# 8-bit weights transposed by VectorE in 32x32 squares where they are rounded, stored so, and loaded straight into one weight tile

## The chip, the cores and the metric

One core of a Trainium2 chip runs the whole program. The metric is device microseconds of that core. The engines are TensorE (PE in the rows; PEld is its weight load), VectorE (DVE), ScalarE (ACT), GpSimd (POOL) and SyncE (SP, which here only issues DMAs and waits).

## The reference

Four layers of cross attention and feed-forward (FFN) on x of 8 sequences x 100 rows x 512, everything in float32. What matters here is the third layer (L2). Its attention part is a recurrence over the context whose result is one 512-vector per sequence, and its FFN rounds weights and activations to 8-bit floats in blocks of 32 along the last axis:

```python
def _mx_dequant(t):
    blocks = t.reshape(rows, feat // 32, 32)
    scales = jnp.maximum(jnp.max(jnp.abs(blocks), axis=-1) / 448.0, 1e-30)
    q = (blocks / scales[..., None]).astype(jnp.float8_e4m3fn).astype(jnp.float32)
    return (q * scales[..., None]).reshape(rows, feat)
def _mx_linear(x2d, w):
    return _mx_dequant(x2d) @ _mx_dequant(w).T
gate, up = _mx_linear(x2d, gate_w), _mx_linear(x2d, up_w)      # gate_w, up_w: 2048 x 512
out = _mx_linear(silu(gate) * up, down_w)                      # down_w: 512 x 2048
```

A weight is rounded in blocks along the axis that the matmul sums over, and TensorE wants that axis on the partitions. So the weights are rounded with this axis along the free dimension and transposed between rounding and use.

## The kernel before

The three weights (12 MB) are cut on the host into 16 **triples** of 128 x 1536: a 128 x 512 piece of the gate, of the up and of the down weight. Class `Triples` rounds them half a triple (128 x 768) at a time, beside stages whose matmuls set the pace: nine triples beside the experts of the first layer (`stage_L0_experts`, 700 to 947 us, names beginning with `e_`), seven beside the spline FFN of the second (`stage_columns_ffn`, 1319 to 1466 us, names `f_`). For half n, DVE takes the blocks' largest values (`scales`, L2685 to L2687), POOL multiplies by the inverse (L2720), DVE takes the exponent (`power`, L2692), ACT lifts it (L2706), DVE rounds by adding and subtracting (`rounding`, L2699 and L2700), and POOL multiplies back in place (`finish`, L2713). DVE's order in the spline FFN is, in each turn of a loop over 16 pairs: two products (L2888) that PE's matmuls and ACT's silu wait for, then `power`, `scales` of the next half, `rounding`. SyncE stores each rounded triple to the DRAM tensor `rounded` (L2675), waits until it is stored, and loads the next into its place (three buffers).

`stage_L2_recurrence` (1466 to 1519 us) adds the recurrence's result to the eight sequences and normalises them. DVE does sequence i in the parts `first`, `shifted`, `second` (L3228, waits for `added`, which ACT makes at L3190 from a PE bank) and `third` (L3239, which completes the sequence and signals `res_made`); SyncE then copies the sequence's rows into the row tiles `s_rows` of the next stage (`into_tiles`, L2080). Beside it the rounded triples come back: SyncE loads a triple into one of four buffers (two named `l_early`, two `l_triple`), PE transposes it in 12 pieces (`turn`, L3308), ACT copies each bank of four into the weight tiles `s_wgu` and `s_wd` (L3200), and SyncE may load the next triple when PE has turned the one before it in the buffer. ACT's one queue holds both the 48 copies and the eight `add_shift` (L3190), in the order that the list `ADD_AT` gives. PE also makes eight `summary` matmuls (L3316) and transposes the last row tile, which DVE has rounded in the recurrence (32 rows, `s_lead`).

Each `nc.Block` ends with a barrier of all engines. The next block, `stage_ffn` (names `f_`, 1519.9 us on), begins with `gate_up(0)` on `s_lead` and the weights (L2217). SyncE meanwhile loads weights of the last layer (L3348). Everything after it depends on this stage.

Of the kernel before, what the change touches and what calls it, by code (L numbers as in the profile page):

```python
# [7 lines left out]
F32 = mybir.dt.float32  # L8
# [8 lines left out]
P = 128  # L17
# [1155 lines left out]
def stage_L0_experts(k, moe, ahead, w_gate, w_up, w_down, raw, rows8, *weights8):  # L1173
# [6 lines left out]
    with ExitStack() as ctx:  # L1180
# [12 lines left out]
        stepped = sem("dve_steps")  # L1193
        b_x, b_g, b_u, b_m, b_y = k.bank[0:2], k.bank[2:4], k.bank[4:6], k.bank[6], k.bank[7]
# [5 lines left out]
        with nc.Block() as block:  # L1200

            @block.sync
            def _(sp):
# [21 lines left out]
                for e in range(NE):  # L1225
# [14 lines left out]
                    if e in STORES_AFTER:  # L1240
                        t = STORES_AFTER[e]
                        triples.store(sp, t)
                        if t + 3 < EARLY_TRIPLES:
                            triples.stored(sp, t)
                            triples.load(sp, t + 3)
                for i in range(2):
                    sp.wait_ge(stored[i], 16 * NE)
                for t in range(EARLY_TRIPLES - 3, EARLY_TRIPLES):
                    triples.stored(sp, t)
# [104 lines left out]
            def _(dve):  # L1354
# [16 lines left out]
                for u in range(U):  # L1371
# [5 lines left out]
                    if u in ROUNDING_UNITS:  # L1377
# [4 lines left out]
                        triples.rounding(dve, step, n)  # L1382
                    if U // 2 <= u < U // 2 + 2 * KC:
                        rows8.vector(dve, (u - U // 2) // KC, (u - U // 2) % KC)
# [730 lines left out]
def stage_ffn(k, tag, gate, up, down, rt, arrived, quantize, block, scales=None, out=None, begin=None, turns=(6, 0, 1, 2, 3, 4, 5), lead=None):  # L2115
# [8 lines left out]
    with ExitStack() as ctx:  # L2124
# [43 lines left out]
        with nc.Block() as program:  # L2168
# [17 lines left out]
            def _(pe):  # L2186
# [18 lines left out]
                def gate_up(u):  # L2205
# [6 lines left out]
                    for w, banks in ((gate, b_g), (up, b_u)):  # L2212
                        for n in range(N):
                            for kc in range(KC):
                                if i == tail:
                                    for s in range(PARTS):
                                        mm = nc.tensor.matmul(banks[u % 2][m * s:m * (s + 1), :], xT[i % 2][:, n, kc, 0:m],  # L2217
                                                              w[:, kc, s * D:(s + 1) * D], start=(kc == 0 and n == 0),
                                                              stop=(kc == KC - 1 and n == N - 1))
                                else:  # L2220
                                    mm = nc.tensor.matmul(banks[u % 2][:], xT[i % 2][:, n, kc, :], w[:, kc, j * D:(j + 1) * D],  # L2221
# [11 lines left out]
                def down_part(u):  # L2233
# [5 lines left out]
                    for n in range(N):  # L2239
                        for kc in range(KC):  # L2240
                            if i == tail:
                                for s in range(PARTS):
                                    mm = nc.tensor.matmul(b_y[i % 2][m * s:m * (s + 1), :], hT[u % 2][:, n, kc, m * s:m * (s + 1)],  # L2243
                                                          down[:, s * KC + kc, :], start=(kc == 0 and n == 0),
                                                          stop=(kc == KC - 1 and n == N - 1))
                            else:
                                mm = nc.tensor.matmul(b_y[i % 2][:], hT[u % 2][:, n, kc, :], down[:, j * KC + kc, :],  # L2247
# [252 lines left out]
def stage_L3_ffn(k, third, out):  # L2500
# [7 lines left out]
    stage_ffn(k, "f3", *third.signs, third.rows, [(arrived[t], 16) if t in arrived else None for t in range(len(TILES))],  # L2508
# [133 lines left out]
STORES_AFTER = {t + 3 if t < 6 else t + 7: t for t in range(EARLY_TRIPLES)}  # L2642


class Triples:
# [4 lines left out]
    def __init__(self, k, ctx, tag, raw, rounded, lo, hi, room):  # L2650
# [4 lines left out]
        self.v, self.c = [sb(f"v{i}", HALF) for i in range(2)], [sb(f"c{i}", HALF) for i in range(2)]  # L2655
# [1541 lines left out]
```

## Time and profile before

| | |
|---|---|
| time, median of 3 runs | 2365.82 us (2358.69 to 2371.73) |
| time of the profiled execution | 2362.94 us |
| span in its trace | 2360.3 us |
| PE busy in the span | 2229.3 us, 94% |
| recurrence stage | 1466.2 to 1519.9 us |

The span runs from the first to the last recorded instruction; 2.6 us of the execution lie outside it. In a row of the timeline a bracket says how long the engine had been idle before the row and what ended that. Times in rows are microseconds from the start of the span, unless ns is written.

### The profile page before, as it was taken

To read this page: it belongs to the slowest core of one execution; us is meant where nothing else is said; L and a number is where in the kernel's file an instruction comes from. 1 tells how busy PE (TensorE), PEld (TensorE's weight loads), DVE (VectorE), ACT (ScalarE), POOL (GpSimd) and SP (SyncE) were. 2 spreads that over 40 slices of the span, in tenths; PEclk is the share of its full clock that TensorE was granted. 3 is DMA by queue.
4 is the path that set the end of the run, shared out by engine and by line. 5 is a ranking of instruction groups with operands and counts; after the bars stand their busy time and mean duration, and the time that the engine had idled before them with its cause. 6 is when DMAs were issued, how large, how long until landed. Compare 5 with 4: busy or idle time off the path is not lost. (4 is left out here: it accounts for less than half of the span.)

```text
span 2360.3 us, 29413 instructions
## 1 busy us (share of the span) xinstructions
PE 2229.3 (94%) x10009; PEld 1186.6 (50%) x10009; DVE 1316.4 (56%) x3393; ACT 803.7 (34%) x2077; POOL 788.5 (33%) x783
## 2 busy tenths in 40 slices
PE   8999999998999999899997899899998899998899
PEld 4455555555445565555554454544443444444454
DVE  5544344214415746467866465776662555656897
ACT  1134444313102212355554222411110456556433
POOL 3665445312403403443322533300000456657100
PEclk9999999998999999899996999899999899999899
DMA  7024400003357864422104622700002211111000
GB/s 204 1 84 148 167 21 13 1 0 128 115 180 273 292 251 160 125 69 69 60 22 145 232 77 82 261 2 9 5 5 78 71 44 58 54 40 52 14 14 15
DMA packets 99803, 214.81 MB, mean 91 GB/s; under 512 B 19332, under 2 KB 40228, under 8 KB 97736
## 3 DMA queue, kind: packets, MB, share of 16 engines
q1 hardware_dynamic: 92232, 195.61, 24.4%
q0 software_dynamic: 7424, 17.32, 2.5%
q8 instruction: 82, 1.34, 0.2%
q14 instruction: 65, 0.53, 0.1%
HBM read 156.75 MB, written 51.18 MB: 88 GB/s over the span
## 5 line engine op out<-in xcount | busy, mean ns | idle before, releaser
L3902 POOL TENSOR_SCALAR a_p<-a_p,a_li 100x257 f32<-100x257 f32 x252 | 187.7, 763 | 110.7 <-DVE a_li L3765 110.7
L638 POOL TENSOR_SCALAR a_shared<-a_shared,a_li 128x361 f32<-128x361 f32 x104 | 131.6, 1265 | 182.3 <-DVE a_li L545 182.3
L3520 PE MATMUL bank<-l_early,a_ctx 128*128 128x512 f32 (+1 forms) x384 | 180.3, 615 | 0.0
L3520 PEld LDWEIGHTS bank<-l_early,a_ctx 128*128 128x128 f32 (+1 forms) x384 | 69.0, 189 | 84.8 <-issue 84.8
L2720 POOL TENSOR_TENSOR e_v<-e_triple,e_inv 128x768 f32<-128x768 f32 x18 | 36.6, 2031 | 218.9 <-DVE e_inv L2687 218.9
L317 PE MATMUL bank<-a_wk,a_ctx 128*128 128x512 f32 (+1 forms) x192 | 94.7, 614 | 9.2 <-DMA a_wk<-in_L_xattn_Wk 5.8
L696 ACT ACTIVATE a_shared<-a_shared,a_nm 128x361 f32<-128x361 f32 x104 | 62.1, 597 | 99.9 <-DVE a_nm L539 99.9
L2438 ACT ACTIVATE f_sg<-bank 128x512 f32<-128x512 f32 x25 | 14.9, 597 | 234.6 <-PE bank L2221 221.7
L2388 POOL TENSOR_TENSOR f_rstd<-f_var,half 128x1 f32<-128x1 f32 (+1 forms) x12 | 7.1, 590 | 258.5 <-DVE f_var L2293 258.5
L2800 PE MATMUL bank<-f_h,s_w 128*128 128x400 f32 x256 | 93.0, 519 | 0.0
L317 PE MATMUL bank<-a_wv,a_ctx 128*128 128x512 f32 (+1 forms) x192 | 90.7, 592 | 0.0
L1596 PE MATMUL bank<-w_ctx,w_wk 128*128 128x361 f32 x256 | 87.7, 487 | 1.7 <-ACT a_kT L1974 1.6
L400 PE MATMUL bank<-a_q_o,a_wq_wo 128*128 128x400 f32 x256 | 88.4, 500 | 0.6 <-issue 0.6
L1302 PE MATMUL bank<-e_wd,e_midT 128*128 128x512 f32 (+1 forms) x192 | 87.9, 593 | 0.6 <-ACT e_midT L1339 0.6
L1604 PE MATMUL bank<-w_wv,w_ctx 128*128 128x512 f32 (+1 forms) x192 | 87.0, 598 | 0.0
L332 PE MATMUL bank<-a_wq_wo,a_shared 128*128 128x512 f32 x192 | 86.5, 594 | 0.0
L2247 PE MATMUL bank<-s_wd,f_hT 128*128 128x512 f32 x192 | 86.2, 593 | 0.0
L537 DVE MEMSET a_hold<- 1x1 f32 x104 | 6.1, 59 | 141.9 <-PE bank L370 125.8
L2221 PE MATMUL bank<-s_wgu,f_xT 128*128 128x512 f32 x192 | 84.6, 594 | 0.7 <-ACTq L2428 0.7
L2221 PE MATMUL bank<-s_wgu,s_lead 128*128 128x512 f32 x192 | 84.4, 593 | 0.0
L1993 ACT ACTIVATE a_p<-a_p,a_nm 100x361 f32<-100x361 f32 x128 | 74.7, 588 | 23.9 <-DVE a_nm L1810 23.6
L1273 PE MATMUL bank<-e_wg,e_xT 128*128 128x352 f32 x256 | 81.1, 460 | 0.8 <-issue 0.5
(494 smaller groups left out, 4918.5 us busy)
## 6 DMA issues: line engine op xcount, KB each, us to landing
slots_x<-zero SPq DMA_DIRECT2D x4, 4096.0 KB, 27.0
s_whole<-in_L_ffn_w SPq DMA_DIRECT2D x24, 512.0 KB, 3.6
e_wg<-in_L_ffn_w_gate SPq DMA_DIRECT2D x16, 704.0 KB, 6.7
e_wu<-in_L_ffn_w_up SPq DMA_DIRECT2D x16, 704.0 KB, 8.0
e_wd<-in_L_ffn_w_down SPq DMA_DIRECT2D x16, 512.0 KB, 4.9
e_xg<-slots_x SPq DMA_DIRECT2D x16, 512.0 KB, 5.2
slots_y<-e_y SPq DMA_DIRECT2D x32, 256.0 KB
a_ctx<-in_ctxT SPq DMA_DIRECT2D x30, 256.0 KB, 3.1
```

The lines of the kernel that those rows point to most:

```text
L317: mm = nc.tensor.matmul(R.bank(name, b, c)[0:m, :], cx[:, kc, lo:lo + m], w[:, kc, :], start=(kc == 0), stop=(kc == KC - 1))
L332: mm = nc.tensor.matmul(bank[:], xnT[:, kc, t * P:(t + 1) * P], wq[:, kc, n * D:(n + 1) * D], start=(kc == 0), stop=(kc == KC - 1))
L400: mm = nc.tensor.matmul(R.bank("y", half, m)[:, 0:BY_HALF * S], wo[:, h, m * P:(m + 1) * P], qo[:, half * BY_HALF:(half + 1) * BY_HALF, h, ...
L638: pool.tensor_scalar(p[s % NP], p[s % NP], li[:, b % 2, h:h + 1], None, ALU.mult).then_inc(normed, 1)
L1302: mm = nc.tensor.matmul(b_y[:], midT[u % 2][0:n, c, :], wd[e % 2][0:n, c, :], start=(c == 0), stop=(c == len(IC) - 1))
L1596: mm = nc.tensor.matmul(R.bank("k", b, n)[:, 0:T], wks[:, kc, n * P:(n + 1) * P], cx[b % 2][:, kc, :], start=(kc == 0), stop=(kc == KC - 1))
L1604: mm = nc.tensor.matmul(R.bank("v", b, c)[0:m, :], cx[b % 2][:, kc, lo:lo + m], wvs[:, kc, :], start=(kc == 0), stop=(kc == KC - 1))
L2221: mm = nc.tensor.matmul(banks[u % 2][:], xT[i % 2][:, n, kc, :], w[:, kc, j * D:(j + 1) * D], start=(kc == 0 and n == 0), stop=(kc == KC - ...
L2247: mm = nc.tensor.matmul(b_y[i % 2][:], hT[u % 2][:, n, kc, :], down[:, j * KC + kc, :], start=(j == 0 and kc == 0 and n == 0), stop=(j == ...
L2800: mm = nc.tensor.matmul(b_y[d][:, 0:GT], down.w[:, f, d * P:(d + 1) * P], h[m % 4][:], start=(f == 0), stop=(f == FC - 1))
L3520: mm = nc.tensor.matmul(bank[0:m, :], columns[:, kc], w[:, kc, :], start=(kc == 0), stop=(kc == KC - 1))
L3902: pool.tensor_scalar(p[g % 2][j][:, lo:hi], p[g % 2][j][:, lo:hi], li[:, h, i:i + 1], None, ALU.mult) \
```

## The change

- A DVE instruction, `turn(n)` (L2696 of the changed kernel), transposes each rounded half triple in its 32x32 squares into a new buffer of its own (two buffers). It stands in DVE's queue after the `rounding` of half n + 1. There are 32 of them, each on 128 x 768 float32.
- The host lays the squares out so that the squares transposed are the whole transposed weight. The `rounded` tensor so holds the weights as the matmuls want them.
- SyncE stores halves (384 KB) in place of whole triples, and no longer waits until a store has landed before it loads the next triple: the buffer is free when both halves are turned.
- In the recurrence PE's 192 transposes and ACT's 48 copies are gone, and so are the two buffers and the loads of the first two triples that had been made beside the spline FFN. SyncE loads all 16 triples straight into one tile `s_weights` of 96 KB a partition, two ahead of each sequence's wait.
- `stage_ffn` takes the weights as views of that tile and waits, ahead of `gate_up(0)`, until all 16 loads have landed (`ready`).

```diff
+    def turn(self, dve, n):
+        dve.wait_ge(self.rounded_made, n + 1)
+        if n >= 2:
+            dve.wait_ge(self.tri_out[n % 2], 16 * (n // 2))
+        dve.transpose(self.turned[n % 2][:], self.half(n)).then_inc(self.half_turned, 1)
...
     def load(self, sp, t):
+        if t >= self.room:
+            sp.wait_ge(self.half_turned, 2 * (t - self.room) + 2)
         sp.dma_start(self.tri[t % self.room][:], self.raw[self.lo + t]).then_inc(self.tri_in[t % self.room], 16)
...
                         triples.rounding(dve, step, i)
+                        if i >= 1:
+                            triples.turn(dve, i - 1)
...
-                early.load_triples(sp, rounded, triples_in)
...
             def _(sp):
-                for t in range(2, FC):
-                    if t >= 4:
-                        sp.wait_ge(turned, 3 * (t - 3))
-                    sp.dma_start(tri[t % 4][:], k.rounded[t]).then_inc(tri_in[t % 4], 16)
-                    if t == B - 1:
-                        sp.wait_ge(res_made, 1)
-                        into_tiles(k, sp, rt, ORDER[0], arrived)
-                for i, b in enumerate(ORDER[1:]):
-                    sp.wait_ge(res_made, i + 2)
+                each_load = FC // B
+                for i, b in enumerate(ORDER):
+                    for t in range(i * each_load, (i + 1) * each_load):
+                        sp.dma_start(whole[:, t * 3:(t + 1) * 3, :].rearrange("p n d -> p (n d)"), k.rounded[t]).then_inc(whole_in, 16)
+                    sp.wait_ge(res_made, i + 1)
                     into_tiles(k, sp, rt, b, arrived)
...
-                add_shift(0)
-                for t in range(FC):
-                    q, j = t // 4, t % 4
-                    for i in range(3):
-                        n = 3 * t + i
-                        act.wait_ge(turned, n + 1)
-                        to = (wgu[:, :, (8 * q + 2 * j + i) * P:(8 * q + 2 * j + i + 1) * P] if i < 2 else
-                              wd[:, 4 * j:4 * j + 4, q * P:(q + 1) * P])
-                        act.copy(to, t_bank[n % 4][:].rearrange("p (c n) -> p c n", c=KC)).then_inc(copied, 1)
-                    if t in ADD_AT:
-                        add_shift(ADD_AT.index(t) + 1)
+                for i in range(B):
+                    add_shift(i)
...
+                if ready:
+                    pe.wait_ge(*ready)
                 for u in range(ahead):
                     gate_up(u)
```

SyncE's queue in the recurrence, before (the part up to the last s_rows copies; 68x512 and 32x512 are the rows of the first sequence done):

```order
L3174 DMA l_triple<-rounded 128x1536 x2
L3174 DMA l_early<-rounded 128x1536 x2
L3174 DMA l_triple<-rounded 128x1536 x2
L2080 DMA s_rows<-res 68x512
L2080 DMA s_rows<-res 32x512
L3174 DMA l_early<-rounded 128x1536 x2
L3174 DMA l_triple<-rounded 128x1536 x2
L3174 DMA l_early<-rounded 128x1536 x2
L3174 DMA l_triple<-rounded 128x1536 x2
L2080 DMA s_rows<-res 100x512
```

and the end of the same queue in the changed kernel, from the copy of the sixth sequence done:

```order
L2082 DMA s_rows<-res 100x512
L3184 DMA s_weights<-rounded 128x1536 x2
L2082 DMA s_rows<-res 12x512
L2082 DMA s_rows<-res 88x512
L3184 DMA s_weights<-rounded 128x1536 x2
L2082 DMA s_rows<-res 40x512
L2082 DMA s_rows<-res 60x512
L3177 UNCONDITIONAL_BRANCH
```

Before, all the loads but the first pair are paced by PE and stand ahead of the last seven sequences' copies. Now each pair stands behind the copies of the sequence before it, and the last pair is the last but one group of the queue.

DVE's queue in the spline FFN, second turn of the loop, in the changed kernel (`f_h` are the products that PE and ACT wait for, `l_b_in` is a small product for the recurrence):

```order
L2717 SCALAR_TENSOR_TENSOR f_v<-f_c,f_v 128x768
L2718 SCALAR_TENSOR_TENSOR f_v<-f_v,f_c 128x768
L2696 STREAM_TRANSPOSE f_turned<-f_triple 128x768
L2929 TENSOR_SCALAR l_b_in<-l_b_in,weight_sum 128x4
L2904 TENSOR_TENSOR f_h<-f_sg,bank 128x400 x2
L2710 TENSOR_SCALAR f_c<-f_v 128x768
L2703 TENSOR_REDUCE f_top<-f_triple 128x24
```

The transpose is new, and the two products stand behind it; the order of the others is as before.

## Rows read from the trace of the kernel before

**Rows 1.** The page: span and busy time of each engine.

```profile
span 2360.3 us, 29413 instructions
...
PE 2229.3 (94%) x10009; PEld 1186.6 (50%) x10009; DVE 1316.4 (56%) x3393; ACT 803.7 (34%) x2077; POOL 788.5 (33%) x783
```

**Rows 2.** Windows: busy us of each engine (count), clock, DMA share, GB/s.

```profile
1466.20:1517.50 51.30, 42.12 (x212) 30.39 (x212) 41.65 (x94) 30.79 (x57) 24.23 (x25) 0.77 0.70 240
...
1492.00:1494.00 2.00, 0.82 (x5) 0.42 (x4) 1.89 (x5) 1.24 (x3) 1.47 (x2) 0.50 1.02 418
1528.40:1800.00 271.60, 266.30 (x734) 122.83 (x734) 170.58 (x319) 31.12 (x57) 2.19 (x4) 1.00 0.04 14
```

**Rows 3.** Lines, 1466 to 1520 us: busy us, mean ns, idle before.

```profile
L3200 ACT COPY s_wgu<-bank 128x512 f32<-128x512 f32 x32 | 17.9, 604 | 11.0 <-PE bank L3308 11.0
L3308 PE MATMUL bank<-ident,l_early 128*128 128x128 f32 x96 | 17.1, 350 | 1.2 <-DMA l_early<-rounded 1.2
```

**Rows 4.** Waits, 1466 to 1520 us: total, times, longest.

```profile
DVE l_early L3228 <- ACT l_early L3190: 4.0, 1, 4.0
...
DVE l_y L3228 <- ACT l_early L3190: 2.9, 2, 2.2
```

**Rows 5.** Timeline of DVE, recurrence: start, us, line.

```profile
1485.79 0.75 DVE L3228 SCALAR_TENSOR_TENSOR l_y<-res,l_rstd,l_early 100x512 f32<-100x512 f32 x1 [2.16 <-ACT l_early L3190]
...
1499.45 0.75 DVE L3228 SCALAR_TENSOR_TENSOR l_early<-res,l_rstd,l_early 100x512 f32<-100x512 f32 x1 [3.96 <-ACT l_early L3190]
...
1515.23 0.75 DVE L3239 SCALAR_TENSOR_TENSOR res<-l_y,l_rstd,l_rb 100x512 f32<-100x512 f32 x1
...
1516.68 0.75 DVE L3239 SCALAR_TENSOR_TENSOR res<-l_y,l_rstd,l_rb 100x512 f32<-100x512 f32 x1
```

**Rows 6.** Timeline of SyncE's DMA issues, recurrence and after.

```profile
1506.06 13.10 SPq L2080 DMA_DIRECT2D s_rows<-res  x12
1519.91 0.35 SPq L3348 DMA_DIRECT2D a_last_ctx<-in_ctx_last_image  x1
```

**Rows 7.** Timeline around the start of the next stage, all engines.

```profile
1519.96 8.41 PE L2217 MATMUL bank<-s_wgu,s_lead 128*32 128x512 f32 x64 [4.96 <-PEq L3167]
...
1526.87 0.69 DVE L2098 TENSOR_TENSOR f_xn<-f_v,f_top 128x512 f32<-128x512 f32 x1
...
1528.31 0.66 PE L2193 MATMUL bank<-ident,f_xn 128*128 128x128 f32 x4
```

**Rows 8.** Tile l_triple: its eight loads of 768 KB.

```profile
DMA to landing us min/median/max: 5.8/7.0/7.8
```

**Rows 9.** Timeline of DVE, rounding beside the spline FFN.

```profile
1344.64 0.55 DVE L2692 TENSOR_SCALAR f_c<-f_v 128x768 int32<-128x768 int32 x1
1345.11 0.94 DVE L2685 TENSOR_REDUCE f_top<-f_triple 128x24 f32<-128x768 f32 x1
...
1401.52 1.05 DVE L2888 TENSOR_TENSOR f_h<-f_sg,bank 128x400 f32<-128x400 f32 x2
...
1407.32 1.04 DVE L2888 TENSOR_TENSOR f_h<-f_sg,bank 128x400 f32<-128x400 f32 x2
...
1428.02 1.05 DVE L2888 TENSOR_TENSOR f_h<-f_sg,bank 128x400 f32<-128x400 f32 x2 [1.23 <-PE bank L2775]
```

**Rows 10.** Timeline of PE in the same stage.

```profile
1346.23 0.95 PE L2775 MATMUL bank<-s_xT,s_gate_up 32*128 32x400 f32 x8
...
1353.36 0.95 PE L2775 MATMUL bank<-s_xT,s_gate_up 32*128 32x400 f32 x8
```

**Rows 11.** Timeline of ACT in the same stage.

```profile
1344.33 0.99 ACT L2856 ACTIVATE f_sg<-bank 128x400 f32<-128x400 f32 x2 [5.54 <-DVE f_h L2888]
...
1350.89 0.50 ACT L2856 ACTIVATE f_sg<-bank 128x400 f32<-128x400 f32 x1 [0.25 <-issue]
```

**Rows 12.** Timeline of DVE and POOL, rounding beside the experts.

```profile
764.50 2.11 DVE L2700 SCALAR_TENSOR_TENSOR e_v<-e_v,e_c 128x768 f32<-128x768 f32 x1
...
769.16 0.69 DVE L1367 COPY e_y<-bank 128x512 f32<-128x512 f32 x1 [2.12 <-PE bank L1302]
```

**Rows 13.** Waits of SyncE at the end of the experts.

```profile
SPq L2678 <- DMA rounded<-e_triple: 3.1, 1, 3.1
```

More of the change, by code:

```diff
@@ L1239, in _ @@
                             triples.load(sp, t)
[L1240 to L1245, printed above, removed]
+                    for n in range(triples.n):
+                        if turned_at(n) // 2 == e:
+                            triples.store(sp, n)
+                            if n % 2 and n // 2 + 3 < EARLY_TRIPLES:
+                                triples.load(sp, n // 2 + 3)
                 for i in range(2):
                     sp.wait_ge(stored[i], 16 * NE)
-                for t in range(EARLY_TRIPLES - 3, EARLY_TRIPLES):
-                    triples.stored(sp, t)
+                triples.stored(sp)
             @block.tensor
@@ L1382, in _ @@
                         triples.rounding(dve, step, n)
+                    for n in range(triples.n):
+                        if turned_at(n) == u:
+                            triples.turn(dve, n)
                     if U // 2 <= u < U // 2 + 2 * KC:
@@ L2112, in quantize_group, with stage_ffn @@
     return dve.scalar_tensor_tensor(y, v, lift, top.unsqueeze(2).to_broadcast(wide), ALU.mult, ALU.mult)
-def stage_ffn(k, tag, gate, up, down, rt, arrived, quantize, block, scales=None, out=None, begin=None, turns=(6, 0, 1, 2, 3, 4, 5), lead=None):
+def stage_ffn(k, tag, gate, up, down, rt, arrived, quantize, block, scales=None, out=None, begin=None, turns=(6, 0, 1, 2, 3, 4, 5), lead=None, ready=None):
     nc = k.nc
@@ L2506, in last_rows @@
         return ()
-    stage_ffn(k, "f3", *third.signs, third.rows, [(arrived[t], 16) if t in arrived else None for t in range(len(TILES))],
+    gate, up, down = third.signs
+    by_unit = lambda w: w.rearrange("p c (j d) -> p c j d", d=D)
+    stage_ffn(k, "f3", by_unit(gate), by_unit(up), down.rearrange("p (j c) d -> p c j d", c=KC), third.rows, [(arrived[t], 16) if t in arrived else None for t in range(len(TILES))],
               quantize_group, GROUP, [third.scale[:, i:i + 1] for i in range(3)], out, last_rows, range(len(TILES)), third.x0)
@@ L2756, in _ @@
                 early.load(sp, recurrence, early_in)
-                early.load_triples(sp, rounded, triples_in)
-                for t in range(FC - EARLY_TRIPLES):
-                    triples.store(sp, t)
-                    triples.stored(sp, t)
-                    if t + 3 < FC - EARLY_TRIPLES:
-                        triples.load(sp, t + 3)
+                for n in range(triples.n):
+                    triples.store(sp, n)
+                    if n % 2 and n // 2 + 3 < FC - EARLY_TRIPLES:
+                        triples.load(sp, n // 2 + 3)
+                triples.stored(sp)
                 sp.wait_ge(early_in, 6 * 16)
-                sp.wait_ge(triples_in, 2 * 16)
             @block.tensor
@@ L2911, in _ @@
                         dve.tensor_scalar(early.binT[:], early.binT[:], k.weight_sum[:, 0:1], None, ALU.mult).then_inc(u_ready, 1)
+                triples.turn(dve, triples.n - 1)
                 for b in range(GB, B):
@@ L3318, in _ @@
                 pe.wait_ge(each_made, 1)
[L3319 removed]
+                for i in range(B):
                     summary(i)
[L3321 to L3326 removed]
                 pe.wait_ge(x_made, 1)
[L3328 removed]
                 for kc in range(KC):
```

80 lines of the change are left out of this document (31 added, 49 removed).

## The prediction

> **What bounds the kernel now.** I read the page first: PE is busy 94% of a span of 2360.3 us [rows 1]. So work taken from PE or ACT is worth time only where PE waits or where a stage ends on another engine. The windows give such a place: in the recurrence (51.3 us) PE is busy 42.1 us at a granted clock of 0.77, DVE 41.7 us, the DMA engines 70% of the time at 240 GB/s; in the FFN behind it (1528.4 to 1800) PE has 266.3 of 271.6 us and the DMA does next to nothing [rows 2]. What is gained ahead of that FFN stays gained, and the same holds for a loss.
>
> Next the waits of the recurrence. DVE waits for ACT's `added` three times, 6.9 us in all [rows 4], and the timeline shows the two long ones, 2.16 us at 1485.79 and 3.96 us at 1499.45 [rows 5]. ACT is late there because its queue also holds the copies (0.60 us each), which themselves wait for PE's transposes [rows 3]. The third wait, 2.9 - 2.16 = 0.74 us, is the first sequence's, where ACT starts as soon as DVE has made the shift; nothing removed stands in its way. The last three rows of DVE and SyncE show how the stage ends: sequence 7 is done at 1515.98, sequence 8 at 1517.43, SyncE issues its last row copies, and the next block's first matmul starts at 1519.96 [rows 5 to 7]. DVE's own chain ends the stage, not the transposes.
>
> **The change in the recurrence.** Of the 192 transposes and 48 copies (a part of each is in [rows 3]) only what DVE waited for counts: 2.16 + 3.96 = 6.12 us. DVE has no other wait there that the change touches, so sequence 7 is done at 1515.98 - 6.12 = 1509.86 and sequence 8 at 1511.31.
>
> SyncE is the next to be late. Between sequence 8 and the next block it issues two row copies and passes the barrier, 1519.96 - 1517.43 = 2.53 us [rows 5, 7]. Now two copies (0.7 us each, an estimate: twelve took 13.10 us with waits in them, 1.1 each at most [rows 6]) and two loads (about 0.4 us each; the next block's load issues at 1519.91 in 0.35 [rows 6]) stand between sequence 7 and the wait for sequence 8: 1509.86 + 1.4 + 0.8 = 1512.1, so 0.8 us behind sequence 8. The block would end, and the next one start, at 1511.31 + 0.8 + 2.53 = 1514.6, that is 5.3 us sooner.
>
> But `gate_up(0)` now also waits for all 16 loads, and the last one is issued at 1509.86 + 1.4 + 0.4 = 1511.7. Loads of this size landed 5.8 / 7.0 / 7.8 us after issue (least, median, most), issued in pairs as here [rows 8]. With the median the weights are there at 1518.7. So PE starts at 1518.7 in place of 1519.96: **1.2 us** of the 5.3 are left; the bounds are 2.4 and 0.4 us. A check from the rate: pairs 7 and 8 are issued from about 1507.4 on, 4 x 0.786 = 3.1 MB. At 418 GB/s, the best that the recurrence shows [rows 2], that takes 7.5 us, at the stage's mean of 240 GB/s 13.1 us; with 1.5 us for the first bytes (an estimate: a landing of 7.0 less two loads at 418 GB/s leaves 3.2, and part of that is queueing) the ends are 1516.4 and 1522, the second a loss of 2.0. The landings, which are of the same size in the same stage, lie between, and I take them.
>
> The DMA rate is where a rule can be weighed. The rows show 418 GB/s over 2 us [rows 2]. The Trainium skill, "DMA: Bandwidth & Descriptors", section "Where 436 GB/s comes from", says that transfers from HBM to SBUF are bound by about 358 GB/s and not by the fabric's 435. This trace disagrees for short stretches; by the page's figure, as an estimate, the four loads take 8.8 us instead of 7.5 and the weights come 1.3 us later than by the row, at 1517.7, still within the bounds of the landings.
>
> PE idles before the next block either way (4.96 us in the row [rows 7]) and begins it on the lower clock either way, so I cost the longer idle at nothing; if it had begun on the high clock before, it would cost up to half of 8.41 us. The first real tile, which DVE normalises at the block's start (7.6 us from 1519.96 to 1527.56 [rows 7]), now starts at 1514.6 and is ready before `gate_up(0)` ends; it was just ready before (PE takes it up at 1528.31), so it adds nothing.
>
> **The new transposes.** 32 instructions on 128 x 768 float32, none in the trace of before. Nearest rows: the one-input reduce of the same tile, 0.94 us; below it the exponent mask, 0.55 us, which is faster than one element a cycle and so a true lower end; above it the rounding beside POOL, 2.11 us [rows 9, 12]. I take 0.95, since the transpose has one input and reads every element once.
>
> Spline FFN (14 of them). PE's turn is 1353.36 - 1346.23 = 7.13 us [rows 10]. DVE's, when nothing holds it, is 1407.32 - 1401.52 = 5.80 us, and once it has caught up it waits 1.23 us for PE in every turn [rows 9]. So there is room for 1.33 us a turn, and 0.95 fits. The products come later by that much. Who waits: ACT's silu, then PE. In the second turn silu ends at 1344.33 + 0.99 = 1345.32, PE needs it at 1346.23: 0.91 us of room; in the third 1351.39 against 1353.36: 1.97 us [rows 10, 11]. The first is short by 0.04 us, nothing. Cost **0**, as long as the transpose takes under 1.33.
>
> Experts (18). DVE waits 2.12 us for PE in each unit after rounding [rows 12]; 0.95 fits, and even 2.11 does. Cost **0**. SyncE now waits for a transpose where it waited for a store to land, about as long, and the experts' loads behind it don't move by more than a microsecond or two. At the end of this stage SyncE waited 3.1 us for the last store of 768 KB [rows 13]. It is 384 KB now: half of 0.786 MB at 418 GB/s is 0.9 us less. **Gain 0.9.**
>
> The first two triples' loads beside the spline FFN disappear; nothing there waited for DMA once it ran, so 0.
>
> **Sum.** 1.2 + 0.9 = 2.1 us off the profiled execution's 2362.94: 2360.8. That execution lies 2.9 us under the median of 2365.82; off the median it is **2363.7 us**. The three runs spread over 13 us, so about 0.5% (11.8 us) is what a measurement can tell from no change. The forecast is no change by that bound.
>
> **Rivals.**
> A: the weights land before the barrier. Then the whole 5.3 + 0.9 = 6.2 us is gained: 2359.6. For it: the best stretch runs at 418 GB/s, and the new loads write one tile with nobody else in the way. Against: the last load is issued 2.9 us before the barrier's end, and no load landed in under 5.8 us [rows 8].
> B, on the other side: the transpose is slow. Above 1.33 us DVE is the bound of the spline FFN. With 2.11 us (the longest row on such a tile) a turn takes 7.94, 0.81 more than PE's; five turns in the first half give 4 us, seven in the second 5.7 less some 3 us of room that the second half starts with: 6.7 us slower, less 2.1: 2370.4. It turns into a net loss from about 1.75 us a transpose. For it: the row of 2.11 is an operation held beside POOL, which runs on the same tile right then. Against: the transpose reads one tensor, and the reduce of one tensor took 0.94 every time. Speaking to this, the Trainium skill, "Vector Engine (DVE) Microarchitecture Reference", section 3.8, has the transpose sustain one element per cycle and lane; no row here shows it, and the sum goes by the reduce.
> C: the loads come late. If the last four move at 240 GB/s, they are there at 1522: 2.0 lost, 0.9 gained, 2366.9. For it: the DMA also carries the row copies, and in the new order two pairs are issued within 4.4 us.
> That the change doesn't do what it says can't be: the queue of PE has no transposes of weights left.
>
> **How the numbers follow.** Chances: forecast 0.64, A 0.12, B 0.14, C 0.10. The range covers A to B with the spread of the runs: 2356 to 2372. None of the cases passes 11.8 us by itself; a faster or slower verdict needs B with over 3 us a transpose, or something not seen. Faster by over 0.5% 0.05, within 0.5% 0.87, slower 0.08.
>
> **What would show it.** Right: no wait of DVE for ACT but the first (0.7 us) in the recurrence; sequence 8 done about 45 us after the stage's start; PE's first FFN matmul held by a DMA of `s_weights` for about 4 us after the barrier; transposes of 0.9 to 1.0 us; DVE still waiting for PE's banks in the late turns of the spline FFN. Wrong: transposes over 1.3 us with PE waiting for silu in every turn; no wait for the weights (A); a wait of 7 us or more (C); or PE waits in the experts, which I hold to be untouched.

## The result: no change that a single run would show, but slower, where faster was forecast

Over 20 runs each, the changed kernel takes 2370.84 us (median; 2367.09 to 2376.64), the kernel before 2365.47 us (2356.56 to 2377.15). The ratio of after to before is 1.0024, 95% interval 1.0013 to 1.0035: 5.7 us slower, 3 to 8. This ratio and those below are the recorded ones, with their intervals; they differ by up to 0.001 from what the two medians divide to. The forecast was 2.1 us faster. Its range held the time, its sign was wrong.

The page of the profiled execution (2367.26 us by itself), against [rows 1]: the span is 5.2 us longer, and PE has less work.

```profile
span 2365.5 us, 29040 instructions
PE 2199.2 (93%) x9817; PEld 1159.6 (49%) x9817; DVE 1340.1 (57%) x3425; ACT 779.4 (33%) x2029; POOL 790.9 (33%) x783
```

The timeline of DVE in the recurrence, its end, against [rows 5]. The stage begins with the copy to `l_each`, at 1466.20 before and at 1469.22 now; all times "into the stage" are counted from it.

```profile
1512.10 0.75 DVE L3236 SCALAR_TENSOR_TENSOR res<-l_y,l_rstd,l_rb 100x512 f32<-100x512 f32 x1
1512.76 0.75 DVE L3234 SCALAR_TENSOR_TENSOR l_y<-l_y,l_stat,l_early 100x512 f32<-100x512 f32 x1
1513.55 0.75 DVE L3236 SCALAR_TENSOR_TENSOR res<-l_y,l_rstd,l_rb 100x512 f32<-100x512 f32 x1
```

Sequence 8 is done 1514.30 - 1469.22 = 45.1 us into the stage; before it was 1517.43 - 1466.20 = 51.2. That is 6.1 us sooner, as forecast from this profile of before. The waits of the same stretch, against [rows 4]: DVE waits for ACT once, and the weights hold PE.

```profile
PE bank L2219 <- DMA s_weights<-rounded: 18.6, 1, 18.6
DVE l_y L3225 <- ACT l_early L3196: 0.8, 1, 0.8
```

SyncE's issues and PE's first FFN matmul, from the timeline, against [rows 6, 7]:

```profile
1510.48 0.96 SPq L3184 DMA_DIRECT2D s_weights<-rounded  x2
1512.88 1.58 SPq L2082 DMA_DIRECT2D s_rows<-res  x2
1514.50 0.99 SPq L3184 DMA_DIRECT2D s_weights<-rounded  x2
1515.53 1.59 SPq L2082 DMA_DIRECT2D s_rows<-res  x2
1517.91 0.35 SPq L3328 DMA_DIRECT2D a_last_ctx<-in_ctx_last_image  x1
...
1525.62 8.85 PE L2219 MATMUL bank<-s_weights,s_lead 128*32 128x512 f32 x64 [18.57 <-DMA s_weights<-rounded]
```

The reader is to see two things. The next block opens 48.7 us into the stage (1517.91), 5.0 sooner than before. And PE begins its work there only 7.7 us after the opening, 56.4 us into the stage; before it began at 53.8. The last two loads of the weights, and their time from issue to landing (least, median, most), from the view of that line:

```profile
L3184 SPq DMA_DIRECT2D s_weights<-rounded x2: 436/471/506, 1514.5 to 1515.1; - x2
DMA to landing us min/median/max: 7.3/8.9/10.5
```

1515.1 + 10.5 = 1525.6: the second load of the last pair lands and PE starts. The forecast had 7.0 us for it. The windows show how full the queues were (columns as in [rows 2]):

```profile
1477.00:1481.00 4.00, 3.81 (x5) 0.83 (x4) 3.13 (x10) 0.69 (x1) 1.22 (x3) 0.50 0.00 0
1489.00:1493.00 4.00, 0.00 (x0) 0.00 (x0) 3.79 (x11) 0.69 (x1) 3.00 (x4) 0.50 1.03 372
1493.00:1497.00 4.00, 0.00 (x0) 0.00 (x0) 3.83 (x10) 0.69 (x1) 3.09 (x4) 0.50 1.00 307
1501.00:1505.00 4.00, 0.00 (x0) 0.00 (x0) 3.73 (x9) 0.46 (x1) 1.31 (x1) 0.50 1.02 357
```

SyncE sends two loads and then waits 12.3 us for sequence 1; in that time the queues fall idle (share 0.00). From 1485 to 1509 the share is 1.0 at 346 GB/s on average: the pace of two loads a sequence is no slower than what the queues carry, so nothing is caught up. Between 1509 and 1513 the queues slacken (share 0.3 to 0.8), and from 1513 to 1525 they are full again, at 334 GB/s.

### The profile page after: what moved, and what is told of

It reads as the page before. It is cut to its first block and busy times, and to the rows that moved or that the text cites. A ratio compares the mean times of both kernels' runs of the same rounds, so it can differ in the third digit from the quotient of the medians.

```text
span 2365.5 us, 29040 instructions
## 1 busy us (share of the span) xinstructions
PE 2199.2 (93%) x9817; PEld 1159.6 (49%) x9817; DVE 1340.1 (57%) x3425; ACT 779.4 (33%) x2029; POOL 790.9 (33%) x783
## 3 DMA queue, kind: packets, MB, share of 16 engines
q8 instruction: 81, 1.33, 0.2%
## 5 line engine op out<-in xcount | busy, mean ns | idle before, releaser
L2249 PE MATMUL bank<-s_weights,f_hT 128*128 128x512 f32 x192 | 86.2, 592 | 0.0
L2223 PE MATMUL bank<-s_weights,f_xT 128*128 128x512 f32 x192 | 84.6, 593 | 0.7 <-ACTq L2432 0.7
L2223 PE MATMUL bank<-s_weights,s_lead 128*128 128x512 f32 x192 | 84.4, 592 | 0.0
```

## The experiments

Each ran beside the kernel before on the same chip, but not all on one chip, so between experiments I compare ratios. Where a ratio is given, 9 to 12 runs stand behind it; the two further executions of the kernel before, the second one of the changed kernel, the doubled transposes and the moved row copies ran once each, for their profiles. The table holds what I compare: lengths in us, each between two events of the same trace. Experts: first raw triple's load to the first load behind the stage. Spline weights: load of `s_terms` to the first load of `f_triple`. Spline FFN: from there to the copy to `l_each`. Then, counted from that copy: the next block's first DMA issue, PE's first FFN matmul, and its first matmul on a full tile. Last, the rest of the FFN: from that matmul to PE's first on the next layer's context (`a_ctx`). In "prefetch late" the next block's first DMA is itself what is held back, so its 55.5 is not the block's opening.

```
                experts weights splineFFN | opens  FFN   full tile | rest
before           244.3   46.6    147.2    | 53.7   53.8   63.5     | 283.9
before again     244.3   46.4    143.0    | 47.6   47.7   59.0     | 285.5
before, third    244.4   46.5    146.9    | 52.2   52.3   62.6     | 282.5
before + turns   244.2   46.3    143.0    | 48.4   48.4   59.3     | 285.2
changed          242.9   48.0    147.2    | 48.7   56.4   66.6     | 282.4
changed again    242.9   47.9    148.0    | 48.9   56.3   66.5     | 282.4
first four       242.2   48.4    147.9    | 47.6   51.0   62.0     | 285.3
prefetch late    242.9   48.4    147.8    | 55.5   55.5   66.0     | 282.6
by use           242.9   48.4    147.9    | 48.7   48.7   59.2     | 282.6
first eight      243.0   48.7    148.0    | 47.6   47.6   58.7     | 285.4
warm wait        243.9   48.6    148.0    | 48.8   56.4   64.8     | 285.8
turn twice       243.1   47.7    150.8    | 48.7   56.4   67.0     | 282.6
copies last      243.0   48.5    147.2    | 55.4   55.5   66.2     | 285.1
eight + warm     243.2   47.9    147.2    | 47.9   47.9   56.9     | 283.7
```

**Four loads ahead.** The edit, in SyncE's program of the recurrence:

```
-                each_load = FC // B
+                LOADS = [4, 2, 2, 2, 2, 2, 2, 0]
                 for i, b in enumerate(ORDER):
-                    for t in range(i * each_load, (i + 1) * each_load):
+                    for t in range(sum(LOADS[:i]), sum(LOADS[:i + 1])):
```

> The changed kernel with the loads of the weights put as 4, 2, 2, 2, 2, 2, 2, 0 ahead of the eight waits for a sequence, in place of 2 each: the last pair goes out behind sequence 6, not 7. Theory 1 (the last pair is late because all DMA queues are full from 16 us into the stage to its end, while they lie idle for the 8 us before): the two extra loads run in the idle 8 us, all 16 have landed about 46 us into the stage, PE is held by the barrier alone and starts the FFN 50 to 51 us into the stage (56.4 in the changed kernel, 53.8 before). That is 6 us off 2370.8, so 2365, and the ratio to the kernel before 1.000. Theory 2 (the time is lost elsewhere: by the transposes, or in the stages between): the start of the FFN moves in the same way, but the ratio stays 1.001 to 1.003.

Measured: 2362.51 us against 2360.39 of the kernel before on this chip, ratio 1.0019 [1.0007, 1.0032]. The FFN starts at 51.0, as expected, but not for the reason given: the weights still hold PE for 3.4 us after the block has opened (47.6), the last load lands 9.2 us after its issue, with no next layer's loads yet issued when it goes out. The full tile comes 4.5 us sooner, but the rest takes 285.3 us in place of 282.4, so 1.6 us are left in the profile; of the 6 us that I expected the ratios show 1.2, less than they can tell apart. Of the 2.9 us taken back, 1.5 lie in the FFN: its stretch up to the next layer's first matmul takes 275.5 to 275.9 us in six of the fourteen profiles, two of them with the recurrence of before, and in each of the six the granted clock falls to 0.50 for 3.4 us some 15 us before its end. In the eight others it takes 274.2 us and the clock doesn't fall there. What sets it, no run shows.

**The next layer's loads held back.**

```
         def prefetch(sp):
+            sp.wait_ge(whole_in, 16 * FC)
             for dst, src in zip([third.last, *early.kv, third.ctx[:]], weights):
```

> The changed kernel with the six loads of the next layer, about 4 MB that go out at the head of the FFN block, held back until all 16 loads of the weights have landed. If the last pair is late because these loads share the queues with it, it lands 7 to 8 us after its issue in place of 10.5, PE starts the FFN 53.5 to 54.5 us into the stage in place of 56.4, and the time is 2368 (2.5 less than the changed kernel). If it is late by what is queued ahead of it, the start stays at 56 to 57 and the time at 2371.

Measured: ratio 1.0030 [1.0015, 1.0045], FFN at 55.5. The last load takes 9.7 us with nothing behind it, 10.5 with the next layer's loads (4.9 MB) beside it:

```profile
L3184 SPq DMA_DIRECT2D s_weights<-rounded x2: 422/464/506, 1513.5 to 1514.1; - x2
DMA to landing us min/median/max: 7.0/8.3/9.7
```

PE starts the FFN 0.9 us sooner, and the ratio shows no gain on the changed kernel. My favoured cause explains 0.8 of 3.5 us. What is ahead of the last load and beside it in the recurrence itself must carry the rest.

**Loads in the order of use, three waits.** The triples' loads go out as 0, 4, 8, 12, 1, 5, ...: the eight that hold gate weights, then four, then four. PE waits for the first eight ahead of the gate half of `gate_up(0)`, for the next four ahead of its up half, for the rest ahead of the first `down_part`:

```
-                        sp.dma_start(... k.rounded[t]).then_inc(whole_in, 16)
+                        sp.dma_start(... k.rounded[t]).then_inc(whole_in[max(0, t % 4 - 1)], 16)
...
-                if ready:
-                    pe.wait_ge(*ready)
...
+                        if u == 0 and ready:
+                            pe.wait_ge(*ready[0 if w is gate else 1])
```

> The changed kernel with the same 16 loads in the order of their use (the eight that hold gate weights, then four, then four) and three waits on PE: gate, up and down, each for its own loads. If PE waits for nothing but the last loads, it starts the FFN about 1 us after the barrier, 50 to 51 us into the stage, with the last loads landing while it multiplies by the gate and up weights: 5.5 to 6 us less than the changed kernel, 2365. Rival: what PE waits for next (the first normalised tile, ready about 7.6 us after the block's start) takes the gain up; then the later work is less than 2 us sooner, 2369.

Measured: 2356.47 against 2360.39 us, ratio 0.9991 [0.9979, 1.0003]. The timeline of PE, where the matmul now waits for the barrier (PEq) and for no DMA:

```profile
1512.74 9.16 PE L2221 MATMUL bank<-s_weights,s_lead 128*32 128x512 f32 x64 [10.88 <-PEq L3179]
```

The copy to `l_each` stands at 1464.04, so this is 48.7 us into the stage, and the full tile follows at 59.2, 7.4 us sooner than in the changed kernel. All loads are issued when they were. So the wait for the last load is worth 7.4 us at the full tile and, by the ratios, 7.8 us of the whole, and without it the changed kernel is level with the kernel before.

**Before, with the transposes added.** Their results are not used.

```
+    def turn(self, dve, n):
+        dve.wait_ge(self.rounded_made, n + 1)
+        dve.transpose(self.turned[n % 2][:], self.half(n)).then_inc(self.half_turned, 1)
```

> The kernel before with DVE's 32x32 transposes added where the change has them (18 beside the experts, 13 beside the spline FFN), their results not used, all else as before. If they are hidden, as the forecast had it: experts and spline FFN as long as before within 1 us, ratio 0.999 to 1.001. If they cost something that the stages' lengths hide from a single trace: 1.001 to 1.003, and then the change's loss would be theirs.

Measured: 2360.41 against 2360.39 us, ratio 1.0009 [0.9995, 1.0022]. Experts 244.2, spline weights 46.3, as without them; the spline FFN is no longer than in any profile of before. The transposes are hidden. But two columns were a surprise: the spline FFN took 143.0 us, and the block opened 48.4 us into a recurrence whose code is that of before, 5.3 sooner than in the profile that the forecast was made from.

**The kernel before, twice more.**

> The kernel before once more, unchanged, for a second profile. The forecast took DVE's two waits for ACT in the recurrence (2.16 and 3.96 us) from one execution. In the run with transposes added, whose recurrence has the same code, they were 0.9 us or less each, and the next block opened 48.4 us into the stage, not 53.8. If they belong to the kernel, they are back here: 5 to 7 us in all, PE starts the FFN at 53 to 55 us into the stage. If they depend on when the clock falls and when loads land, they are something between 0 and 6 us here, and the FFN starts at 48 to 54.

> The kernel before, unchanged, for a third profile of its own. In two of three executions with its recurrence the FFN began 47.7 and 48.4 us into the stage, in the one that the forecast was made from 53.8; the spline FFN took 143.0, 143.0 and 147.2 us. If the forecast's profile was the odd one: 47 to 49 and 143. If both happen about as often: either.

Measured: the FFN starts at 47.7 and 52.3, the spline FFN takes 143.0 and 146.9 us; so both kinds come up. The waits of DVE for ACT in the recurrence, of the second profile:

```profile
DVE l_y L3228 <- ACT l_early L3190: 0.8, 1, 0.8
```

and of the third:

```profile
DVE l_y L3228 <- ACT l_early L3190: 4.4, 2, 3.7
DVE l_early L3228 <- ACT l_early L3190: 1.0, 1, 1.0
```

Against 6.9 us in the forecast's profile [rows 4]. Less the first sequence's, the wait that the change removes is 6.1, 4.7 or 0 us. The windows of eight microseconds beside it, of the second profile:

```profile
1470.30:1478.30 8.00, 7.74 (x60) 6.47 (x60) 6.98 (x19) 7.99 (x17) 4.43 (x5) 1.00 0.84 286
```

and of the third, at the same place of the stage:

```profile
1475.50:1483.50 8.00, 8.00 (x30) 6.07 (x30) 7.00 (x19) 3.91 (x7) 4.45 (x6) 0.50 0.48 176
```

With PE granted 1.00 (2.4 GHz) it does 60 matmuls in 7.74 us and ACT keeps its copies moving; with 0.50 (1.2 GHz) it does 30 in 8.00, and ACT, and through it DVE, are late afterwards. The forecast's profile has 0.53 there and 33 matmuls. That the clock makes the difference is read from three executions; no run set it. Over the four profiles with this recurrence the FFN starts at 50.5 us on average, not at 53.8.

**Eight loads ahead.** As the first edit, with `LOADS = [8, 2, 2, 2, 2, 0, 0, 0]`.

> The changed kernel with the loads of the weights put as 8, 2, 2, 2, 2, 0, 0, 0. With 4 ahead the FFN began 51.0 us into the stage, still held by the weights for 3.4 us after the barrier. If SyncE's 8 idle microseconds and the pace of 2 a sequence are what makes the weights late, eight loads land in the first 16 us, the last pair is issued 28 us into the stage and lands by 40, PE waits for the barrier alone and starts at 48.7 as with the order of use, 7.7 us sooner than the changed kernel: 2357 on the scale of this comparison, ratio 0.999. Rival: the row copies of the first sequences land behind the loads and DVE's measuring of the last tile waits for them; then the barrier itself comes later than 49 us into the stage.

Measured: 2359.53 against 2360.47 us, ratio 0.9998 [0.9987, 1.0009]. The block opens at 47.6 and PE starts with it. The last load landed 42.4 us into the stage, not by 40, early enough all the same. The rival's stall of DVE does not show. Two ways of taking the wait away give 47.6 and 48.7; the 1.1 us between them I put down to SyncE's last pair of issues, which in this version, as with four ahead (47.6 too), is gone from behind sequence 7 (the forecast had 0.8 for it).

**Matmuls ahead of the wait.**

```
                 if ready:
+                    for _ in range(24):
+                        nc.tensor.matmul(k.bank[7][:, 0:P], k.ident[:], k.ident[:], start=True, stop=True)
                     pe.wait_ge(*ready)
```

> The changed kernel with 24 small matmuls of the identity, into a bank that nobody reads, on PE ahead of its wait for the weights. The forecast costed PE's longer idle at nothing. If the clock is high when the weights land, the first group of FFN matmuls (8.85 us in the changed kernel, 9.2 to 9.7 in the others) takes 4.5 to 5.5 us and PE takes up the first full tile 3.5 to 4 us sooner, since that tile has been normalised by then: ratio to before 1.001 in place of 1.0024. If the group is not bound by the clock, or the clock falls later instead, nothing changes: 1.002 to 1.003.

Measured: 2365.81 against 2360.47 us, ratio 1.0015 [1.0003, 1.0026]. From PE's timeline (each of the small matmuls is two records there):

```profile
1520.40 7.62 PE L2264 MATMUL bank<-ident 128*128 128x128 f32 x48 [11.00 <-PEq L3179]
1527.95 7.07 PE L2219 MATMUL bank<-s_weights,s_lead 128*32 128x512 f32 x64
```

The small matmuls lasted 7.6 us, just as long as the weights took, and PE comes to the group when it does in the changed kernel. The group takes 7.07 us in place of 8.85, not the 4.5 to 5.5 that I expected. Two windows of the changed kernel show why:

```profile
1525.00:1529.00 4.00, 3.38 (x16) 0.80 (x20) 1.16 (x5) 0.00 (x0) 0.00 (x0) 0.50 1.03 420
1529.00:1533.00 4.00, 4.00 (x40) 1.16 (x36) 0.00 (x0) 0.00 (x0) 0.00 (x0) 0.97 1.02 420
```

There PE begins the group at 0.50 (1.2 GHz, 16 matmuls) and has 1.00 (2.4 GHz, 40 matmuls) from about 1529 on: 3.5 us at half the rate cost 1.8. The full tile comes 1.8 us sooner. So the idle ahead costs the changed kernel 1.8 us up to there. In this profile the rest takes it back (285.8 in place of 282.4), but the profile is of the slowest of the twelve runs, 2372.7 us; whether the whole kernel keeps the gain, the ratios (1.0015 and 1.0024) can't say.

**Each transpose twice.**

```
+        dve.transpose(self.turned[n % 2][:], self.half(n)).then_inc(self.once, 1)
+        dve.wait_ge(self.once, n + 1)
         dve.transpose(self.turned[n % 2][:], self.half(n)).then_inc(self.half_turned, 1)
```

> The changed kernel with each of DVE's 32x32 transposes done twice, 1.9 us a turn. The forecast put the room of a turn at 1.33 us in the spline FFN and at 2.12 us in the experts. If so, DVE is the bound in the spline FFN: the stretch from its first load to the recurrence takes 3 to 5 us more than the changed kernel's 147.2, and PE waits there for silu in the middle turns; the experts stay within 1 us. If the room is larger, both stay.

Measured: spline FFN 150.8 us, 2.8 to 3.6 more than the two profiles of the changed kernel; experts 243.1 as there. In the middle turns PE now waits 0.5 us for silu, from its timeline:

```profile
1416.76 0.95 PE L2793 MATMUL bank<-s_xT,s_gate_up 32*128 32x400 f32 x8 [0.48 <-ACT f_sg L2874]
1424.43 0.95 PE L2793 MATMUL bank<-s_xT,s_gate_up 32*128 32x400 f32 x8 [0.48 <-ACT f_sg L2874]
```

A turn takes 1424.43 - 1416.76 = 7.67 us where it took 7.13. The second transpose adds 0.98 us, of which 0.54 is paid. The two together are 1.94 us, so 1.40 found room, where the forecast had 1.33.

**Row copies behind the loads.**

```
                     sp.wait_ge(res_made, i + 1)
+                    if i == 0:
+                        into_tiles(k, sp, rt, b, arrived)
+                for b in ORDER[1:]:
                     into_tiles(k, sp, rt, b, arrived)
```

> The changed kernel with the row copies of sequences 2 to 8 moved behind the last pair of loads on SyncE; the waits for the sequences stay, so that the loads go out at the same points. SyncE then issues 11 or more copies of 0.8 us each at the end, so the block opens 8 or 9 us later; what counts is the time from issue to landing. In the changed kernel the second load of a pair takes 7.9 to 11.4 us, from the second pair on, and the rate falls from above 400 to below 300 GB/s in the stretches in which copies run. If the copies take the loads' time in the queues, the second load of each pair lands 6 to 7 us after issue here, the last too (10.5 in the changed kernel), and the rate stays above 380 GB/s. If the loads slow each other, or the memory is slow at that place, it stays at 8 to 11.

Measured: the block opens at 55.4, from the copies' issues. The last load:

```profile
L3184 SPq DMA_DIRECT2D s_weights<-rounded x1: 434/434/434, 1514.0 to 1514.0; - x1
DMA to landing us min/median/max: 7.5/7.5/7.5
```

7.5 us in place of 10.5. But this edit takes away two things: as the block opens only at 55.4, the next layer's loads too go out behind the landing (51.5). The fair comparison is with those loads held back, 9.7 us: the copies are worth 2.2. The rate over a window, with loads alone, and then with the copies beside the last two loads:

```profile
1491.00:1494.00 3.00, 0.00 (x0) 0.00 (x0) 2.90 (x7) 0.69 (x1) 2.45 (x3) 0.50 0.98 403
1512.00:1515.00 3.00, 0.00 (x0) 0.00 (x0) 2.93 (x5) 0.00 (x0) 1.13 (x2) 0.50 1.00 393
1515.00:1518.00 3.00, 0.00 (x0) 0.00 (x0) 0.05 (x1) 0.00 (x0) 0.00 (x0) 0.50 1.03 377
```

Some loads in the middle still took 8.2 and 8.5 us, so the expectation of 6 to 7 for each is not met; but the largest landing fell from 11.4 to 8.5 and the median of all 16 from 7.3 to 6.3. The small copies, 12 of 24 to 200 KB, cost the last load 2.2 us. The loads also went out up to 1.8 us sooner than in the changed kernel, since no copy's issue stood before them.

**The changed kernel once more.**

> The changed kernel, unchanged, for a second profile. The start of its FFN is set by the landing of the last load: 56.4 us into the stage within 0.3, as in the first profile and in the run with doubled transposes, whatever the clock does. The spline FFN takes 147 to 148 us in all six profiles of its kind so far; here too, if that belongs to the kernel, 143 if it is chance.

Measured: 56.3, and 148.0 (56.4 and 147.2 in the first profile). Both as expected.

**Eight loads ahead and a busy PE.** The loads of the sixth experiment, and behind the transposes of the last tile, PE's last work in the recurrence:

```
                 mm.then_inc(x_turned, 1)
+                for _ in range(32):
+                    nc.tensor.matmul(t_bank[1][:, 0:P], k.ident[:], k.ident[:], start=True, stop=True)
```

> The loads as 8, 2, 2, 2, 2, 0, 0, 0 and 32 small matmuls of the identity on PE behind its last work in the recurrence, so that it starts the FFN at 47.6 us into the stage after work and not after 10 idle microseconds. If the clock is high then, the first group takes 5 to 7 us in place of 9.8, and the first full tile, ready about 55.3 us into the stage, is the next to be waited for: PE takes it up at 56.5 to 57.5 in place of 58.7, ratio 0.9985 to 0.9995. If what is gained there is lost where the clock falls later, as with the matmuls ahead of the wait: ratio 0.9995 to 1.0005.

Measured: 2360.95 against 2365.78 us, ratio 0.9974 [0.9960, 0.9989]: the one version that is faster than the kernel before, by 6.2 us (2.6 to 9.5), and, by the ratios, than the changed kernel. PE's timeline:

```profile
1507.85 9.82 PE L3313 MATMUL bank<-ident 128*128 128x128 f32 x64
1517.96 7.07 PE L2219 MATMUL bank<-s_weights,s_lead 128*32 128x512 f32 x64 [0.30 <-PEq L3177]
1525.62 0.66 PE L2195 MATMUL bank<-ident,f_xn 128*128 128x128 f32 x4 [0.59 <-DVE f_xn L2100]
```

The full tile is taken up at 56.9 us into the stage. PE now waits 0.59 us for DVE's first normalised tile, so the weights and PE hold nothing up at this place. The ratio is better than the 0.9985 to 0.9995 that I expected: against eight loads alone it is 5.7 us less, of which the full tile gives 1.8 and the rest (283.7 in place of 285.4) 1.7. The remaining 2 us are less than the two intervals can tell.

## Why the prediction was wrong

**The step that failed** is "with the median the weights are there at 1518.7", a landing of 7.0 us that was 10.5. The last load was issued when forecast: 1515.1 - 1469.22 = 45.9 us into the stage, forecast 1511.7 - 1466.2 = 45.5. The 7.0 stands on "loads of this size landed 5.8 / 7.0 / 7.8 us after issue, issued in pairs as here", and both halves of that are misread. The view is of the tile `l_triple` alone, where the trace gives the landing of four loads. And after the first pair, before's loads went out 0.8 to 5.6 us apart, as PE freed the buffers, while the changed kernel's last pair goes out 4 us behind another pair, with two row copies between and two behind. The same trace has a load into `l_early`, issued behind another load and the first two row copies:

```profile
L3174 SPq DMA_DIRECT2D l_early<-rounded x1: 795/795/795, 1484.8 to 1484.8; - x1
DMA to landing us min/median/max: 9.0/9.0/9.0
```

With 9.0 us the weights would have been there at 1520.7, a start of the FFN 0.7 us later than before, and the forecast would have had the other sign at this place.

Of the 3.5 us too many, the next layer's loads carry 0.8 (10.5 against 9.7) and the row copies 2.2 (9.7 against 7.5). The remaining 0.5, with neither in the way, I put down to the pair ahead; no run took that away.

Rival C had the landing: four loads at the stage's mean rate, weights there at 1522, that is 55.8 us into the stage. Measured: 56.4 and 56.3, and its sign, a wait of 7 us or more, came true with 7.7. From the issue of the seventh pair to the last landing is 15.1 us for 3.1 MB, or 231 GB/s with the forecast's 1.5 us for the first bytes. The queues moved 312 GB/s in that time; C's rate is what the copies, the next layer's loads and the slack around 1511 left for the weights. C had a chance of 0.10, because I held a landing of the same size in the same stage to be better evidence than a rate. It is, if the queue ahead of it is as full.

**The base was off too.** The 6.12 us of DVE's waits were real in the profile that I worked from, and they are gone in the changed kernel. But the kernel before has them, in whole or in most part, in only two of its three profiles, and its version with transposes has 0.9 us beyond the first sequence's. Against the average of four the block opens not 5.0 but 1.7 us sooner, the FFN starts not 2.6 but 5.8 us later, and the full tile comes 66.5 - 61.1 = 5.4 us later. One profile's waits were taken for the kernel's.

**That the range held the time** is no merit of the mechanism: its upper end came from rival B, a slow transpose, and the transposes took 0.97 us.

**PE's longer idle time** was costed at nothing, and that held: the group of 64 matmuls takes 8.85 and 8.88 us after it, and in the four profiles with the idle of before it took 8.4 to 10.0. What idling costs at all is 1.8 us (7.07 after work), and before paid it as well. The bound I gave, half of 8.41, took those 8.41 us for time at the low clock; the 7.07 at 1.00 say that most of it was at the high one.

**Right:** SyncE falls behind by its last pair (block opens 5.0 sooner in the profiles at hand, forecast 5.3); the last half-size store at the end of the experts (0.9 forecast; SyncE's wait for it is 2.2 us in place of 3.1 [rows 13], the stage 1.4 shorter); the transposes, 0.97 us each (0.95 forecast) and hidden in both stages, rival B out; the room of 1.33 us a turn, 1.40 by doubling them. DVE's wait of 1.23 us in the late turns [rows 9] shrank to 0.23 and 0.35 us, with 0.97 of it filled:

```profile
1436.96 0.97 DVE L2696 STREAM_TRANSPOSE f_turned<-f_triple 128x768 f32<-128x768 f32 x1
1438.15 1.05 DVE L2904 TENSOR_TENSOR f_h<-f_sg,bank 128x400 f32<-128x400 f32 x2 [0.23 <-issue]
```

**The account of the whole.** Averages of the two profiles of the changed kernel less those of the four with the stages of before: experts -1.4, spline weights +1.5, spline FFN +2.6, up to the full tile +5.4, rest of the FFN -1.9: 6.2 us, where the runs say 5.7. That they agree so well is partly chance: the spans of these profiles differ by 7.4 us, because stretches whose code is the same don't cancel either (+3.1 ahead of the experts, -1.4 between the experts and the spline weights, -0.6 at the end). The first and fourth are explained above. For the others I can show no cause in the edits:

- The spline weights stage took 47.7 to 48.7 us in all ten profiles with the change, 46.3 to 46.6 in all four without. Its code is the same. In eight of the ten POOL's first wait in it, for the load of `s_powers`, is about 1 us longer (4.2 to 4.7 us, against 3.1 to 3.5); in the other two it is 3.1 and 3.6 and the stage is long all the same. What does part the two kinds is the granted clock: it comes back to 1.00 24.4 to 25.0 us into the stage in the four, 26.3 to 28.0 in the ten. The transposes don't do it (46.3 with them). The cause stays open.
- The spline FFN took 147.2 to 148.0 in nine profiles with single transposes, and 143.0, 143.0, 146.9, 147.2 without the rest of the change. The windows 60 and 80 us into it, of the changed kernel:

```profile
1382.00:1392.00 10.00, 10.00 (x48) 6.99 (x47) 0.00 (x0) 1.53 (x6) 0.00 (x0) 0.87 0.23 81
...
1402.00:1412.00 10.00, 7.18 (x37) 4.06 (x36) 9.78 (x15) 2.00 (x4) 3.54 (x2) 0.83 0.00 0
```

and of before with transposes:

```profile
1379.50:1389.50 10.00, 10.00 (x53) 7.23 (x52) 0.00 (x0) 1.53 (x6) 0.00 (x0) 1.00 0.16 65
...
1399.50:1409.50 10.00, 8.37 (x48) 4.40 (x48) 9.83 (x17) 3.65 (x6) 3.94 (x3) 1.00 0.19 78
```

PE's clock falls in the one and not in the other. So it is in all thirteen profiles, the one of doubled transposes left out: in each of the eleven where this stage took 146.9 us or more the clock falls twice there, about 80 and 60 us before the stage's end, and in the two where it took 143.0 not once. The later start of the stage's work, by 1.5 us, isn't needed for it, since two of the eleven are of the kernel before; what else decides it, no run shows. It could make the change's loss partly one of when the clock falls.

## What to carry to other kernels

When a change turns many small waits into one wait for the last transfer, the landing time must be taken from transfers in equally full queues, or worked out from bytes over the stage's mean rate; a median from emptier queues is the optimistic end. Look at all transfers of that size in the trace, not at one buffer's. Send such loads while the queues are idle, ahead of the first wait on their issuing engine, and let the consumer wait for the part it uses first: these cures were worth 7.4 to 7.9 us at the next full tile and 6.1 and 7.8 us of the whole time. And take a wait that a profile shows at two or three executions before you book it as gain: this one was 0.8 to 6.9 us.

## What was not expected of the hardware

- Row copies of 24 to 200 KB from SBUF to SBUF, 1.6 MB beside 12.6 MB of loads, slow loads out of proportion. With loads alone the queues moved 394 GB/s over 15 us (1487 to 1502, row copies behind the loads); in the changed kernel, with the copies between, 349 over 19 us (1487 to 1506), copies' bytes included, and 307 in its slowest window shown. The share is full in all of them.
- Loads alone ran at 393 to 403 GB/s over 3 us, and the next layer's loads at 420 over 8 us (1525 to 1533). The Trainium skill, "DMA: Bandwidth & Descriptors", section "Where 436 GB/s comes from", says that transfers from HBM are bound at about 358 GB/s, its figure for each of two cores; the trace, of one core, does not agree over such stretches. With the copies in, the changed kernel's windows read 307 to 372 GB/s, but they hold copies too and say nothing on such a bound.
- A 32x32 transpose of 128 x 768 float32 takes 0.965 to 0.972 us in all 32 cases, about the pace of the one-input reduce (0.94).
- In one kernel the clock falls in the same stage of one execution and not of another: 33 or 60 matmuls in the same eight microseconds of the recurrence. The block then opens at 52.2 and 53.7 us or at 47.6 and 48.4, and the spline FFN takes 4 us more or less: this is as large as what the change does.
